# A graph-attention kernel whose edge rows come from two engines: all 31 columns of every batch fetched by GpSimd

## The chip, the cores and the metric

The kernel runs on one core of one Trainium2 chip. The metric is the device time in microseconds (us) of one execution, measured without a profiler. The profile shown here is of one further execution.

## The reference, cut to what matters

6250 nodes with 256 features and 206250 edges, sorted by destination. A layer norm, two graph-attention convolutions, a layer norm, an add, and then a mixture of 8 experts of which each node takes two.

```python
def _gat_conv(x, W, att_src, att_dst, bias, src, dst):
    xw = (x @ W).reshape(N, H, CPH)                   # N = 6250, H = 8, CPH = 16
    a_s = jnp.einsum('nhc,hc->nh', xw, att_src)
    a_d = jnp.einsum('nhc,hc->nh', xw, att_dst)
    e = jax.nn.leaky_relu(a_s[src] + a_d[dst], 0.2)
    m = jax.ops.segment_max(e, dst, num_segments=N)
    p = jnp.exp(e - m[dst])
    s = jax.ops.segment_sum(p, dst, num_segments=N)
    return jax.ops.segment_sum(xw[src] * (p / s[dst])[:, :, None], dst, num_segments=N).reshape(N, H * CPH) + bias
x = x + layernorm(concat(conv0, conv1) + layernorm(x)) * gamma + beta
x = x + top-2-of-8 experts: w * (gelu(xf @ W1[e] + b1[e]) @ W2[e] + b2[e])
```

For the change only `xw[src]` matters: for every edge, the row of its source node (128 features and 8 scores, 136 floats, 544 bytes).

## The kernel before, in words

A prologue (to some 285 us of the profile) normalises and projects all nodes, stores the rows of both convolutions in the DRAM tensor `tables`, and finds where each node's edges begin. The first 6272 edges are then done in four pieces. The other 1563 columns of 128 edges (one edge of each partition's chunk) go through 51 batches: 50 of 31 columns, the last of 13.

A batch `b` has one of three slots `G[slot(b)]` in SBUF. GpSimd (POOL) fetches its rows in `gather` (line 877), one indirect DMA of 128 rows for each column (line 882). It waits for the index list, and for the store of the batch that had the slot before, `b - 3`. VectorE (DVE) does `marks` and `scan_batch` (lines 1674 to 1713): the scores and their running maximum, the product of weights and rows (line 1701), and nine scans along the edges (1705, 1708). ScalarE (ACT) makes the exponentials (1101, 1103, 1110) and in `copy_back` (1084, 1124) turns the sums back into the slot. SyncE (SP) then issues the loads for batch `b + 3` and the store of the slot to `state` (line 661). Within an engine the order is the order of the program; between engines it is set by semaphores.

In batches 10 to 49 POOL fetches only the first 28 columns. The last three come from TensorE (PE). The table of the first convolution is loaded in SP's batch 5 (line 703) into `room`, and DVE splits it in `split_table` before batches 8 and 9 into an upper and a lower part that lie in SBUF where `X`, the node features, was. For this, SP stores `X` to DRAM (`xkept`, line 694, batches 1 to 7) and loads it again after the batches (`reload`, line 726). `code_columns` turns source nodes into codes, which SP spreads over the partitions for each batch (line 652). ACT compares them with the node numbers in `mark_stretch` (lines 1155 and 1159: 17 levels in four stretches) into one-hot matrices. PE multiplies these by the table in `columns` (line 1299): 17 levels x 3 columns x 2 parts = 102 products a batch, into three PSUM banks. DVE picks out the right third in `take_columns` (lines 1771 and 1773), nine instructions ahead of `marks`.

After the batches, POOL fetches the last state of each node (`last_states1`, `last_states2`; it waits for PE's `levels_used` before them), DVE, ACT and PE combine, normalise and route seven groups of nodes, and 105 tiles of tokens go through the experts (lines 1390 and 1396).

Of the kernel before, what the change touches and what calls it, by code (L numbers as in the profile page):

```python
# [23 lines left out]
I32 = mybir.dt.int32  # L24
ALU = mybir.AluOpType
# [50 lines left out]
FIX = 5  # L76
# [6 lines left out]
CODES_AT = 8704  # L83
# [5 lines left out]
PEC = 3  # L89
PARTS = 2  # L90
PE0, PE1 = 10, NB - 1
TABLE_AT = 5
SPLIT_AT = 8
NPC = PEC * (PE1 - PE0)
LEV = 17
TPL = 3
MIDDLE = float(LEV * P // 2)
UPPER_BITS = -(1 << 12)
SPLITS = (((0, 13), (13, 12)), ((25, 12), (37, 12)))
LEVEL_ORDER = (0, LEV - 1, *range(1, LEV - 1))  # L100
STRETCHES = ((0, 5), (5, 9), (9, 13), (13, 17))
FIX_B = 7

assert SLOTS % 2 == 1 and FIX_B + 1 < PE0 - 1
assert NBLK * BLK == E and NG * GRP == NT and (NB + NA) % NS == 1 and sum(CO) == J1 and max(CO) * 2 * ROWS <= J * ROWS
assert CL + 1 <= WA and PEC < CL and 2 * HD * WA <= HL and 2 * ROWS * WA <= ROWS * L and ZT % ZJ == 0 and ZT * P == EP
# [6 lines left out]
def build(nc, x, src, dst, W0, as0, ad0, b0, W1, as1, ad1, b1, gamma, beta, Wg, bg, eW1, eb1, eW2, eb2, out):  # L113
    ctx = ExitStack()
    with ctx:
# [20 lines left out]
        xkept = dram("xkept", [NG, P, GRP * D])  # L136
        code_type = mybir.dt.float16
        codes = dram("codes", [NPC, P], code_type)
# [7 lines left out]
        room_at = -(-(SBUF_TOP - nc.sbuf_bytes_remaining) // 32) * 32  # L146
        room = sb("room", [P, ROOM])
        arena_at = -(-(SBUF_TOP - nc.sbuf_bytes_remaining) // 32) * 32
# [13 lines left out]
        rounded = mybir.dt.float32r  # L162
        part_size = NT * ROWT
        table_parts = nc.alloc_sbuf_tensor_at("table_parts", [P, PARTS, part_size], rounded, offset=arena_at + 4 * XO, align_bytes=4)
        onehot = nc.alloc_sbuf_tensor_at("onehot", [P, LEV, PEC * P], rounded, offset=room_at, align_bytes=4)
        at = FB + PARTS * part_size - NT * D
        column_codes = [a.bitcast(code_type) for a in (AR[:, at:at + PEC * P // 2], room[:, CODES_AT:CODES_AT + PEC * P // 2])]
        assert at + PEC * P // 2 <= FB + 1152 and LEV * PEC * P <= CODES_AT and CODES_AT + PEC * P // 2 <= ROOM and LEV * TPL >= NT
# [45 lines left out]

        tile_pick = sb("tile_pick", [P, NPC, TPL])
        src_code = tile_pick.rearrange("p n q -> p (n q)")[:, 0:NPC]
        code_out = room[:, NT * ROWT:NT * ROWT + NPC // 2].bitcast(code_type)
        minus_code = sb("minus_code", [P, LEV])
# [75 lines left out]
        codes_loaded = [sem(f"codes_loaded{s}") for s in range(2)]  # L294
        levels_used = sem("levels_used")
        columns_taken = sem("columns_taken")
        parts_ready = sem("parts_ready")
        rows_copied = sem("rows_copied")
        cleared_then_node_half = sem("cleared_then_node_half")
        links_then_codes_ready = sem("links_then_codes_ready")  # L300
# [29 lines left out]
        marked_by_act = sem("marked_by_act")  # L330
# [50 lines left out]
        def by_pe(b):  # L381

            return PE0 <= b < PE1

        def pe_columns(b):

            return PEC if by_pe(b) else 0

        def fetched_columns(b):

            return cols(b) - pe_columns(b)

# [20 lines left out]
        def gather_count(b):  # L413

            return piece_count(NA - 1, slot(b)) + 16 * sum(fetched_columns(q) for q in range(b % NS, b + 1, NS))
# [50 lines left out]
        column_banks = (ps[1], ps[5], ps[6])  # L466
# [12 lines left out]

        staging = room[:, 0:part_size]  # L480
# [100 lines left out]
        def _(sp):  # L581
            with nc.allow_non_contiguous_dma(reason="small tables, once"):
# [52 lines left out]
                flat_codes = codes.rearrange("c p -> (c p)")  # L635

# [9 lines left out]
                def fetch_codes(b):  # L646
                    if b == PE0:
                        sp.wait_ge(lists_stored, 32)
                        sp.wait_ge(x_rows_stored, 16 * NG)
                        sp.wait_ge(biased_stored, 16 * NG)  # L650
                    n = PEC * (b - PE0) * P
                    sp.dma_start(column_codes[b % 2], flat_codes[n:n + PEC * P].partition_broadcast(P)).then_inc(codes_loaded[b % 2], 16)

                def fetch_and_store(b):
                    sp.wait_ge(rows_copied, NA + b + 1)
                    if by_pe(b + NS):
                        fetch_codes(b + NS)
                    if b + NS < NB:
                        fetch(b + NS)
                    s, n = slot(b), cols(b)  # L660
                    sp.dma_start(states0[:, b * J * ROWS:(b * J + n) * ROWS], G[s][:, 0:n, :].rearrange("p j r -> p (j r)")).then_inc(batch_stored[s], 16)
# [27 lines left out]
                for b in range(NB):  # L689
                    if 1 <= b < PEEL:  # L690
                        g = b - 1
                        sp.wait_ge(biased_ready, 2 * (g + 1))
                        sp.dma_start(hbd[g], norm_again.rearrange("p t d -> p (t d)")).then_inc(biased_stored, 16)
                        sp.dma_start(xkept[g], X[:, g * GRP:(g + 1) * GRP, :].rearrange("p t d -> p (t d)")).then_inc(x_rows_stored, 16)
                    if b == TABLE_AT:
                        sp.wait_ge(x_rows_stored, 16 * TABLE_AT)
                        sp.wait_ge(adstart_cleared, 16 * (ZT // ZJ))
                        sp.wait_ge(zeros_then_pads_stored, 16)
                        sp.wait_ge(adst_stored, 16)
                        for q in range(RB):  # L700
                            sp.wait_ge(row_stored[q], 16 * (-(-(NT - q) // RB)))
                        sp.wait_ge(degrees_moved_then_table_loaded, 32)
# [22 lines left out]
                def reload(g):  # L725
                    sp.dma_start(X[:, g * GRP:(g + 1) * GRP, :].rearrange("p t d -> p (t d)"), xkept[g]).then_inc(x_loaded[g], 16)

# [6 lines left out]
                for g in range(2):  # L734
                    reload(g)
# [3 lines left out]
                for g in range(NG):  # L739
# [3 lines left out]
                    if g + 2 < NG:  # L743
                        reload(g + 2)
# [6 lines left out]
                    if g >= 1:  # L751
                        sp.wait_ge(x_rows_stored, 16 * (NG + g))
# [16 lines left out]
                sp.wait_ge(x_rows_stored, 32 * NG)  # L769
# [36 lines left out]
        def _(pool):  # L806
# [15 lines left out]
            g.iota(minus_code[:, :], pattern=[[-P, LEV]], base=int(MIDDLE), channel_multiplier=-1, allow_small_or_imprecise_dtypes=True)  # L822
# [54 lines left out]
            def gather(b):  # L877
# [3 lines left out]
                for j in range(fetched_columns(b)):  # L881
# [3 lines left out]
            def gather_fix_rows(n):  # L885
                if n == 0:
                    pool.wait_ge(links_then_codes_ready, 2)
                else:
                    pool.wait_ge(fix_rows_stored, 16 * n)
# [35 lines left out]
            pool.wait_ge(levels_used, len(STRETCHES) * (PE1 - PE0))  # L925
# [49 lines left out]
        def _(act):  # L975
# [129 lines left out]
            def batch_decays(b, w=L):  # L1105
# [39 lines left out]
            def mark_stretch(b, i):  # L1145

                n, (first, end) = b - PE0, STRETCHES[i]
                if i == 0:
                    act.wait_ge(parts_ready, len(SPLITS))
                    act.wait_ge(codes_loaded[b % 2], 16 * (n // 2 + 1))  # L1150
                if n >= 1:
                    act.wait_ge(levels_used, len(STRETCHES) * (n - 1) + i + 1)
                for a in range(first, end):
                    v = LEVEL_ORDER[a]
                    last = S.activation(onehot[:, a, :], column_codes[b % 2], ACT.Abs, bias=minus_code[:, v:v + 1])  # L1155
                last.then_inc(marked_by_act, 1)
                count = 2 * (len(STRETCHES) * n + i) + 1
                act.wait_ge(marked_by_act, count)
                S.activation(onehot[:, first:end, :], onehot[:, first:end, :], ACT.Relu, bias=1.0, scale=-1.0).then_inc(marked_by_act, 1)  # L1159

            def whole_batch(b, w=L, next_w=L):
                if 1 <= b < PEEL:
                    normalise_again(b - 1)
                if b == PE0 - 1:
                    mark_stretch(b + 1, 0)
                    mark_stretch(b + 1, 1)
# [5 lines left out]
                if by_pe(b + 2) and b + 2 > PE0:  # L1172
                    mark_stretch(b + 2, 1)
# [81 lines left out]
        def _(pe):  # L1255
# [38 lines left out]
            def product(bank, mark, a, k):  # L1294

                v = LEVEL_ORDER[a]
                w = TPL * ROWT
                z = min(w, NT * ROWT - v * w)
# [962 lines left out]
```

## Time and profile before

| what | value |
|---|---|
| time, median of 3 runs | 3143.54 us (3141.79 to 3145.52) |
| span of the profiled execution | 3949.4 us |
| columns fetched by POOL in batches (line 882) | 1443 |
| columns from PE | 120 |
| busy in the span: PE, DVE, ACT, POOL | 49%, 52%, 40%, 49% |
| first gather of a batch, start of the last | 285.3 us, 2789.5 us |

The profiled execution has no other time on record than its span, which is 806 us above the median of the runs. In the rows, times are from the start of the span; "idle before" is how long the engine had been idle, and behind the arrow stands what released it. "issue" is idle time for which the profile shows no wait.

### The profile page before, as it was taken

The numbers are of one execution on the slowest core, as the hardware profiler recorded it, in microseconds if no ns is written. First come the engines' busy times: TensorE is split into PE (matmuls) and PEld (weight loads), VectorE is DVE, ScalarE is ACT, GpSimd is POOL, SyncE is SP. The second block draws the span as 40 slices with busy tenths as digits, with TensorE's granted clock in tenths as the row PEclk, the third lists the DMA queues.
The fourth block names the chain that finished last, engine by engine and source line by source line (L and its number), as shares of the span: only waits on it lengthen the run. The fifth ranks groups of instructions, "written<-read, shape, count | busy, mean of one in ns | idle before, by whom it ended". The sixth has DMA issues, their size and how long they took to land.

```text
span 3949.4 us, 38354 instructions
## 1 busy us (share of the span) xinstructions
PE 1918.5 (49%) x10116; PEld 1741.9 (44%) x10117; DVE 2043.1 (52%) x4266; ACT 1578.9 (40%) x2552; POOL 1927.4 (49%) x1920
## 2 busy tenths in 40 slices
PE   4500000134435354453544454545213489999998
PEld 2400000123425344353544453435213389999998
DVE  5465676625527355363554563545687544444443
ACT  4322223315536355453555554445323323333332
POOL 4467657645554555535555555465466612222222
PEclk8755555556767676676677776766655599999999
DMA  8244449313332333323333333233365622222222
GB/s 299 76 117 135 144 161 155 120 42 94 94 94 86 94 93 92 94 80 96 94 96 92 94 92 93 59 99 93 119 220 179 230 42 37 36 36 37 36 36 32
DMA packets 212942, 396.68 MB, mean 100 GB/s; under 512 B 76396, under 2 KB 164785, under 8 KB 206305
## 3 DMA queue, kind: packets, MB, share of 16 engines
q1 hardware_dynamic: 136049, 245.72, 18.4%
q0 software_dynamic: 75664, 149.21, 16.8%
q8 instruction: 41, 0.67, 0.1%
q10 hardware_dynamic: 1120, 0.52, 0.0%
q14 instruction: 68, 0.56, 0.0%
HBM read 203.53 MB, written 191.78 MB: 100 GB/s over the span
## 4 chain that ended last, share of the span: by engine, by line
PE 34%; issue 25%; DVE 16%; DVEq 10%; another core or an unknown queue 8%; ACT 4%; SPq 1%; POOL 1%; DMA 1%; POOLq 0%; ACTq 0%
PE ps L1299 13%; PE ps L1390 9%; PE ps L1396 9%; DVEq L1703 5%; DVE AR L1708 4%; PE ps L1270 1%; ACT onehot L1155 1%; ACT AR L1084 1%; DVEq L1709 1%; DVE AR L1773 1%; POOL AR L882 1%; DVE group_stats L1945 1%; ACT onehot L1159 1%; PE ps L1381 1%
## 5 line engine op out<-in xcount | busy, mean ns | idle before, releaser
L882 POOL DMA_INDIRECT AR<-tables,idx x1443 | 1377.0, 954 | 1095.5 <-DMA state<-AR 620.8
L1299 PE MATMUL ps<-table_parts,onehot 128*128 128x408 f32 (+1 forms) x4080 | 953.7, 388 | 1218.1 <-issue 752.5
L1299 PEld LDWEIGHTS ps<-table_parts,onehot 128*128 128x128 f32 x4080 | 861.9, 221 | 1309.9 <-issue 949.7
L1771 DVE TENSOR_SCALAR AR<-ps,tile_pick 128x136 f32<-128x136 f32 x120 | 35.4, 351 | 991.2 <-PE ps L1299 555.4
L1084 ACT COPY AR<-AR 128x1984 f32<-128x1984 f32 (+3 forms) x110 | 392.0, 3564 | 355.1 <-DVE AR L1708 195.6
L956 POOL DMA_INDIRECT out<-AR,idb x105 | 183.5, 1748 | 597.6 <-issue 560.1
L1708 DVE TENSOR_TENSOR_SCAN AR<-ps,AR 128x512 f32<-128x512 f32 x404 | 454.2, 1197 | 0.0
L1390 PEld LDWEIGHTS ps<-AR 128*128 128x128 f32 x3360 | 393.9, 193 | 6.6 <-DVE AR L2164 1.3
L1390 PE MATMUL ps<-AR 128*128 128x128 f32 x3360 | 394.5, 276 | 0.9 <-DVE AR L2164 0.9
L1701 DVE TENSOR_TENSOR AR<-AR,ps 128x3968 f32<-128x3968 f32 (+1 forms) x51 | 356.7, 6994 | 20.7 <-ACT AR L1103 13.4
L1101 ACT ACTIVATE ps<-AR 128x248 f32<-128x248 f32 (+1 forms) x51 | 19.2, 376 | 702.4 <-DVE AR L1688 411.4
L1155 ACT ACTIVATE onehot<-AR,minus_code 128x384 fp32r<-128x384 f16 x340 | 180.2, 603 | 265.6 <-remote 253.7
L2164 DVE COPY AR<-AR 128x1024 f32 x210 | 151.4, 721 | 208.7 <-PE ps L1390 207.2
L1159 ACT ACTIVATE onehot<-onehot 128x1536 fp32r<-128x1536 f32 (+1 forms) x160 | 250.6, 1566 | 5.1
L1243 ACT ACTIVATE AR<-ps,bcur 128x128 f32<-128x128 f32 x424 | 121.2, 369 | 258.6 <-PE ps L1390 258.5
L1243 ACT ACTIVATE room<-ps,bcur 128x128 f32<-128x128 f32 x416 | 119.0, 368 | 254.1 <-PE ps L1390 254.1
L1155 ACT ACTIVATE onehot<-room,minus_code 128x384 fp32r<-128x384 f16 x340 | 180.1, 604 | 67.1 <-remote 59.0
L1396 PE MATMUL ps<-AR 128*128 x848 | 191.9, 379 | 1.3 <-DVE AR L2207 1.3
L1396 PE MATMUL ps<-AR,room 128*128 x832 | 188.2, 379 | 0.0
L1396 PEld LDWEIGHTS ps<-AR 128*128 128x128 f32 x848 | 157.0, 190 | 20.8 <-issue 1.7
L1396 PEld LDWEIGHTS ps<-AR,room 128*128 128x128 f32 x832 | 154.0, 190 | 18.8
L1326 PE MATMUL ps<-ident,sml 128*128 128x128 f32 x6 | 2.4, 501 | 319.7 <-DVE sml L1845 319.7
(345 smaller groups left out, 2352.4 us busy)
## 6 DMA issues: line engine op xcount, KB each, us to landing
state<-AR SPq DMA_DIRECT2D x50, 2232.0 KB
AR<-tables,idx POOLq DMA_INDIRECT x1492
AR<-in_L_ffn_W SPq DMA_DIRECT2D x16, 1024.0 KB
AR<-placed SPq DMA_DIRECT2D x105, 130.0 KB, 2.0
adstart<-room SPq DMA_DIRECT2D x26, 496.0 KB
AR<-adstart SPq DMA_DIRECT2D x50, 248.0 KB
tables<-AR SPq DMA_DIRECT2D x49, 136.0 KB
room<-tables SPq DMA_DIRECT2D x14, 476.0 KB
```

Source lines behind the costliest of these rows:

```text
L882: pool.indirect_dma_start(out=G[s][:, j, 0:ROWT], out_offset=None, in_=table_rows, in_offset=bass.IndirectOffsetOnAxis(ap=idx[:, s, j:j + ...
L956: pool.indirect_dma_start(out=out, out_offset=bass.IndirectOffsetOnAxis(ap=idb[:, s, :], axis=0), in_=ys[:, s, :], in_offset=None, bounds_ ...
L1084: return S.copy(to.rearrange("p j (h c) -> p j h c", h=HD)[:, :, :, a:z], of[:, :, 1:n + 1].rearrange("p (c h) j -> p j h c", h=HD)[:, :, ...
L1155: last = S.activation(onehot[:, a, :], column_codes[b % 2], ACT.Abs, bias=minus_code[:, v:v + 1])
L1159: S.activation(onehot[:, first:end, :], onehot[:, first:end, :], ACT.Relu, bias=1.0, scale=-1.0).then_inc(marked_by_act, 1)
L1243: last = S.activation(hsT[s][:, m, :], ps[2 * s + h][:, (m % 4) * P:(m % 4 + 1) * P], ACT.Gelu, bias=bcur[:, s, m:m + 1])
L1299: return T.matmul(bank[:, 0:z], mark, table_parts[:, k, v * w:v * w + z], start=(a == 0 and k == 0), stop=(a == LEV - 1 and k == PARTS - 1))
L1390: mm = T.matmul(ps[2 * s + h][:, m * P:(m + 1) * P], w1_cur[:, k, (h * 4 + m) * P:(h * 4 + m + 1) * P], xsT[:, s, k, :], start=(k == 0), s ...
L1396: mm = T.matmul(ps[5][:, 0:D], hsT[s][:, m, :], AR[:, bass.ds(e * (MH * D) + (NEX * KD * HID + m * D), D)], start=(m == 0), stop=(m == MH ...
L1701: V.tensor_tensor(TS[:, 0:F, js].rearrange("p (c h) j -> p c h j", h=HD), rows_in[:, :, 0:F].rearrange("p j (h c) -> p c h j", h=HD), bc(W ...
L1703: dd()
L1708: V.tensor_tensor_scan(T2[:, i * step:(i + 1) * step], decays(w), T2[:, i * step:(i + 1) * step], 0.0, ALU.mult, ALU.add).then_inc(entry_u ...
```

## The change

`by_pe`, `pe_columns` and `fetched_columns` go, and `gather` issues `cols(b)` indirect DMAs in every batch. `mark_stretch`, `product`, `columns`, `code_columns`, `take_columns`, `split_table` and every call and semaphore of theirs go. `X` stays in its place in SBUF: its store to `xkept` and its reload go, and the loads of the table and of the codes. The order of all that remains is as before.

```diff
-                for j in range(fetched_columns(b)):
+                for j in range(cols(b)):
                     pool.indirect_dma_start(out=G[s][:, j, 0:ROWT], out_offset=None, in_=table_rows,
...
-            return piece_count(NA - 1, slot(b)) + 16 * sum(fetched_columns(q) for q in range(b % NS, b + 1, NS))
+            return piece_count(NA - 1, slot(b)) + 16 * sum(cols(q) for q in range(b % NS, b + 1, NS))
...
                     sp.wait_ge(rows_copied, NA + b + 1)
-                    if by_pe(b + NS):
-                        fetch_codes(b + NS)
                     if b + NS < NB:
...
                         sp.dma_start(hbd[g], norm_again.rearrange("p t d -> p (t d)")).then_inc(biased_stored, 16)
-                        sp.dma_start(xkept[g], X[:, g * GRP:(g + 1) * GRP, :].rearrange("p t d -> p (t d)")).then_inc(x_rows_stored, 16)
-                    if b == TABLE_AT:
...
-                        sp.dma_start(staging.rearrange("p (t r) -> p t r", r=ROWT), tab[0].rearrange("(t p) r -> p t r", p=P)).then_inc(degrees_moved_then_table_loaded, 16)
-                    if b == FIX + 1:
-                        sp.wait_ge(links_then_codes_ready, 3)
-                        sp.dma_start(codes.rearrange("c p -> p c"), code_out).then_inc(lists_stored, 16)
                     if b == NB - 1:
-                        sp.wait_ge(levels_used, len(STRETCHES) * (PE1 - PE0))
...
-            pool.wait_ge(levels_used, len(STRETCHES) * (PE1 - PE0))
             for n in range(4):
                 last_states2(n)
...
-                if by_pe(b + 1):
-                    mark_stretch(b + 1, 2)
-                    mark_stretch(b + 1, 3)
...
-                    if half == 0 and by_pe(b + 2) and b + 2 > PE0:
-                        mark_stretch(b + 2, 0)
...
-                if by_pe(b + 2) and b + 2 > PE0:
-                    mark_stretch(b + 2, 1)
...
-            pe.wait_ge(parts_ready, len(SPLITS))
-            for b in range(PE0, PE1):
-                for i in range(len(STRETCHES)):
-                    columns(b, i)
             chain(2)
...
             def whole_batch(b, w=L, next_w=L):
-                if SPLIT_AT <= b < SPLIT_AT + len(SPLITS):
-                    split_table(b - SPLIT_AT)
-                if by_pe(b):
-                    take_columns(b)
...
-                    if g + 2 < NG:
-                        reload(g + 2)
...
-                dve.wait_ge(x_loaded[g], 48 if g == NG - 1 else 32)
+                dve.wait_ge(x_loaded[g], 32 if g == NG - 1 else 16)
```

## Rows read from the trace of the kernel before

**Rows 1.** The page: busy time of each engine, share of the span, instructions.
```profile
PE 1918.5 (49%) x10116; PEld 1741.9 (44%) x10117; DVE 2043.1 (52%) x4266; ACT 1578.9 (40%) x2552; POOL 1927.4 (49%) x1920
```

**Rows 2.** Who waited for whom, whole span: us in total, times, longest.
```profile
PE ps L1299 <- issue: 752.5, 322, 54.2
...
POOL AR L882 <- DMA state<-AR: 620.8, 24, 58.1
...
DVE AR L1771 <- PE ps L1299: 555.4, 18, 89.4
```

**Rows 3.** Line 882: ns min/median/max; idle before it; who waited for it.
```profile
L882 POOL DMA_INDIRECT AR<-tables,idx x1443: 942/947/2572, 285.3 to 2789.5; - x181
...
  issue: 474.6, 1419
...
  DVE AR L1680: 4.5, 1
```

**Rows 4.** POOL in order of time: start, us, instruction, idle before.
```profile
743.26 2.55 POOL L882 DMA_INDIRECT AR<-tables,idx  x1 [0.30 <-issue]
...
848.44 0.95 POOL L882 DMA_INDIRECT AR<-tables,idx  x1 [0.30 <-issue]
849.69 0.94 POOL L882 DMA_INDIRECT AR<-tables,idx  x1 [0.30 <-issue]
908.72 0.94 POOL L882 DMA_INDIRECT AR<-tables,idx  x1 [58.08 <-DMA state<-AR]
...
1003.35 0.95 POOL L882 DMA_INDIRECT AR<-tables,idx  x1 [24.89 <-DMA state<-AR]
```

**Rows 5.** PE in order of time: products that come singly, and in a run.
```profile
814.82 0.50 PE L1299 MATMUL ps<-table_parts,onehot 128*128 128x408 f32 x1 [2.30 <-issue]
817.62 0.50 PE L1299 MATMUL ps<-table_parts,onehot 128*128 128x408 f32 x1 [2.30 <-issue]
...
866.84 21.05 PE L1299 MATMUL ps<-table_parts,onehot 128*128 128x408 f32 x102 [3.01 <-DVE AR L1773]
```

**Rows 6.** DVE in order of time: batches 10 and 12.
```profile
871.28 0.41 DVE L1692 COPY AR<-ps 128x248 f32<-128x248 f32 x1
...
872.67 7.25 DVE L1701 TENSOR_TENSOR AR<-AR,ps 128x3968 f32<-128x3968 f32 x1
...
931.64 6.98 DVE L1701 TENSOR_TENSOR AR<-AR,ps 128x3968 f32<-128x3968 f32 x1 [0.63 <-issue]
```

**Rows 7.** All engines in order of time: batches 3, 4 and 5, with 31 fetched columns.
```profile
505.18 6.80 DVE L1701 TENSOR_TENSOR AR<-AR,ps 128x3968 f32<-128x3968 f32 x1
...
525.19 1.03 ACT L1124 COPY AR<-AR 128x496 f32<-128x496 f32 x1
...
545.78 6.80 DVE L1701 TENSOR_TENSOR AR<-AR,ps 128x3968 f32<-128x3968 f32 x1
...
580.03 6.79 DVE L1701 TENSOR_TENSOR AR<-AR,ps 128x3968 f32<-128x3968 f32 x1
```

**Rows 8.** DVE in order of time, behind batch 0.
```profile
379.55 0.28 DVE L1830 TENSOR_SCALAR fix_at<-fix_at 128x1 f32<-128x1 f32 x3 [5.87 <-issue]
```

**Rows 9.** POOL and DVE in order of time, around the end of the batches.
```profile
2820.30 0.95 POOL L919 DMA_INDIRECT room<-state,node_index  x1 [29.90 <-PE ps L1299]
...
2860.31 0.17 DVE L1672 COPY carry<-AR 128x16 f32<-128x16 f32 x1
```

**Rows 10.** SyncE in order of time: the store of batch 12's slot.
```profile
994.24 0.43 SPq L661 DMA_DIRECT2D state<-AR  x1
```

**Rows 11.** The chain that ended last, a piece of the combining stage.
```profile
3117.10 13.12 another core or an unknown queue
```

**Rows 12.** Groups of instructions: busy us, mean ns, idle before.
```profile
L1159 ACT ACTIVATE onehot<-onehot 128x1536 fp32r<-128x1536 f32 (+1 forms) x160 | 250.6, 1566 | 5.1
...
L1790 DVE TENSOR_TENSOR table_parts<-room 128x1632 fp32r<-128x1632 f32 (+1 forms) x4 | 7.5, 1884 | 0.0
...
L2069 DVE TENSOR_TENSOR AR<-AR 128x1792 f32<-128x1792 f32 x7 | 14.2, 2026 | 0.5
```

More of the change, by code:

```diff
@@ L75 @@
 AW = 38048
-FIX = 5
 BIASED_IN = ((0, 2), (0, 2), (1, 2), (1, 2), (2, 1), (3, 2), (3, 2))
@@ L82 @@
 ROOM = 9088
-CODES_AT = 8704
 AHEAD = 2 * GRP
@@ L88 @@
 ZFIRST = 14
[L89 to L101, printed above, removed]
 FIX_B = 7
-assert SLOTS % 2 == 1 and FIX_B + 1 < PE0 - 1
+assert SLOTS % 2 == 1 and FIX_B + 2 < NB - 2
 assert NBLK * BLK == E and NG * GRP == NT and (NB + NA) % NS == 1 and sum(CO) == J1 and max(CO) * 2 * ROWS <= J * ROWS
-assert CL + 1 <= WA and PEC < CL and 2 * HD * WA <= HL and 2 * ROWS * WA <= ROWS * L and ZT % ZJ == 0 and ZT * P == EP
+assert CL + 1 <= WA and 2 * HD * WA <= HL and 2 * ROWS * WA <= ROWS * L and ZT % ZJ == 0 and ZT * P == EP
 def bc(ap, shape):
@@ L135, in build @@
         placed = dram("placed", [NEX * REG + P + 2 * P, ROWP])
-        xkept = dram("xkept", [NG, P, GRP * D])
-        code_type = mybir.dt.float16
-        codes = dram("codes", [NPC, P], code_type)
         states0 = state[0][NP:EP, :].rearrange("(p j) r -> p (j r)", p=P)
@@ L143, in build @@
         adstart_c = adstart[NP:EP, :].rearrange("(p j) r -> p (j r)", p=P)
-        room_at = -(-(SBUF_TOP - nc.sbuf_bytes_remaining) // 32) * 32
         room = sb("room", [P, ROOM])
-        arena_at = -(-(SBUF_TOP - nc.sbuf_bytes_remaining) // 32) * 32
         AR = sb("AR", [P, AW])
@@ L160, in build @@
         FB = XO + NT * D
[L162 to L168, printed above, removed]
         zero = room[:, 0:1024]
@@ L213, in build @@
         bcur = sb("bcur", [P, 2, MH])
[L215 to L218, printed above, removed]
         hrow = room[:, 5520:6032].rearrange("p (s d) -> p s d", s=2)
@@ L293, in build @@
         searched_by_act = sem("searched_by_act")
[L294 to L297, printed above, removed]
         rows_copied = sem("rows_copied")
         cleared_then_node_half = sem("cleared_then_node_half")
-        links_then_codes_ready = sem("links_then_codes_ready")
+        links_ready = sem("links_ready")
         last_states_spread = sem("last_states_spread")
@@ L329, in build @@
         places_ready = sem("places_ready")
-        marked_by_act = sem("marked_by_act")
         pads_then_tiles_ready = sem("pads_then_tiles_ready")
@@ L379, in build @@
             assert any(GRP * (g + 1) - 1 in counted_at(t) for t in range(count_step(g))) or g == 0
[L381 to L391, printed above, removed]
         def slot(b):
@@ L465, in build @@
         same = cut(5820, C)
-        column_banks = (ps[1], ps[5], ps[6])
         VIEW = {}
@@ L478, in build @@
         degree_rows = share_of.rearrange("p a b c t h -> p (a b c t h)")[0:NT, 0:P]
-        staging = room[:, 0:part_size]
         def repeats(w):
@@ L633, in _ @@
                     load_piece_adst(q)
-                flat_codes = codes.rearrange("c p -> (c p)")
                 def fetch_adst(b):
@@ L644, in fetch @@
                     fetch_adst(b)
[L646 to L652, printed above, removed]
                 def fetch_and_store(b):
                     sp.wait_ge(rows_copied, NA + b + 1)
-                    if by_pe(b + NS):
-                        fetch_codes(b + NS)
                     if b + NS < NB:
@@ L693, in _ @@
                         sp.dma_start(hbd[g], norm_again.rearrange("p t d -> p (t d)")).then_inc(biased_stored, 16)
-                        sp.dma_start(xkept[g], X[:, g * GRP:(g + 1) * GRP, :].rearrange("p t d -> p (t d)")).then_inc(x_rows_stored, 16)
-                    if b == TABLE_AT:
[L696 to L702, printed above, removed]
-                        sp.dma_start(staging.rearrange("p (t r) -> p t r", r=ROWT), tab[0].rearrange("(t p) r -> p t r", p=P)).then_inc(degrees_moved_then_table_loaded, 16)
-                    if b == FIX + 1:
-                        sp.wait_ge(links_then_codes_ready, 3)
-                        sp.dma_start(codes.rearrange("c p -> p c"), code_out).then_inc(lists_stored, 16)
                     if b == NB - 1:
-                        sp.wait_ge(levels_used, len(STRETCHES) * (PE1 - PE0))
                         for i in range(NOWN):
@@ L723, in down_in @@
                     sp.dma_start(w2s[:, e, :, :], eW2[e].rearrange("(m p) d -> p m d", p=P)).then_inc(expert_weights_loaded, 16)
-                def reload(g):
-                    sp.dma_start(X[:, g * GRP:(g + 1) * GRP, :].rearrange("p t d -> p (t d)"), xkept[g]).then_inc(x_loaded[g], 16)
                 own(3)
@@ L733, in _ @@
                 own(5)
-                for g in range(2):
-                    reload(g)
                 for g in (5, 6):
@@ L751, in _ @@
                     if g >= 1:
-                        sp.wait_ge(x_rows_stored, 16 * (NG + g))
+                        sp.wait_ge(x_rows_stored, 16 * g)
                     sp.dma_start(out[g * GRP * P:(g + 1) * GRP * P, :].rearrange("(t p) d -> p t d", p=P), X[:, g * GRP:(g + 1) * GRP, :]).then_inc(x_rows_stored, 16)
@@ L767, in _ @@
                 sp.dma_start(placed[NEX * REG:NEX * REG + P, :], padrow[:, :]).then_inc(zeros_then_pads_stored, 16)
-                sp.wait_ge(x_rows_stored, 32 * NG)
+                sp.wait_ge(x_rows_stored, 16 * NG)
                 for i in range(3):
@@ L821, in _ @@
             g.iota(e8[:, :], pattern=[[1, HD]], base=0, channel_multiplier=0, allow_small_or_imprecise_dtypes=True)
-            g.iota(minus_code[:, :], pattern=[[-P, LEV]], base=int(MIDDLE), channel_multiplier=-1, allow_small_or_imprecise_dtypes=True)
             g.memset(padrow[:, :], 0.0)
@@ L886, in gather_fix_rows @@
                 if n == 0:
-                    pool.wait_ge(links_then_codes_ready, 2)
+                    pool.wait_ge(links_ready, 2)
                 else:
@@ L1143, in _ @@
                 copy_piece_back(q)
[L1145 to L1159, printed above, removed]
             def whole_batch(b, w=L, next_w=L):
@@ L1163, in whole_batch @@
                     normalise_again(b - 1)
-                if b == PE0 - 1:
-                    mark_stretch(b + 1, 0)
-                    mark_stretch(b + 1, 1)
                 batch_weights(b, w)
@@ L1292, in _ @@
             project(NT - 1)
[L1294 to L1298, printed above, removed]
-                return T.matmul(bank[:, 0:z], mark, table_parts[:, k, v * w:v * w + z], start=(a == 0 and k == 0), stop=(a == LEV - 1 and k == PARTS - 1))
-            def columns(b, i):
-                n, (first, end) = b - PE0, STRETCHES[i]
-                if i == 0 and n >= 1:
-                    pe.wait_ge(columns_taken, n)
-                pe.wait_ge(marked_by_act, 2 * (len(STRETCHES) * n + i + 1))
-                for a in range(first, end):
-                    for c in range(PEC):
-                        for k in range(PARTS):
-                            mm = product(column_banks[c], onehot[:, a, c * P:(c + 1) * P], a, k)
-                mm.then_inc(levels_used, 1)
             pe.wait_ge(edge_lists_used, 1)
@@ L1321, in chain @@
                 pe.wait_ge(last_states_spread, n + 1)
-                pe.wait_ge(links_then_codes_ready, 1)
+                pe.wait_ge(links_ready, 1)
                 if n >= 1:
@@ L1518, in edge_marks @@
                 V.tensor_copy(dstF, dstI)
-                V.tensor_copy(src_code[:, :].rearrange("p (b c) -> p b c", c=PEC),
-                              srcI[:, PE0 * J:PE1 * J].rearrange("p (b j) -> p b j", j=J)[:, :, J - PEC:J])
                 V.tensor_copy(dst1[:, :], idx1[:, 1, :])
@@ L1733, in _ @@
             edge_columns(VIEW[L, HD])
-            def code_columns():
-                tile, of_level, at_ = cut(0, NPC), cut(NPC, NPC), cut(2 * NPC, NPC)
-                dd()
-                V.tensor_scalar(tile, src_code[:, :], 1.0 / P, 0.5 / P - 0.5, ALU.mult, ALU.add)
-                dd()
-                V.tensor_scalar(tile, tile, MAGIC, None, ALU.add)
-                dd()
-                V.tensor_scalar(tile, tile, MAGIC, None, ALU.subtract)
-                dd()
-                V.tensor_scalar(of_level, tile, 1.0 / TPL, -1.0 / TPL, ALU.mult, ALU.add)
-                V.scalar_tensor_tensor(at_, tile, -float(P), src_code[:, :], ALU.mult, ALU.add)
-                dd()
-                V.tensor_scalar(of_level, of_level, MAGIC, None, ALU.add)
-                dd()
-                V.tensor_scalar(of_level, of_level, MAGIC, None, ALU.subtract)
-                dd()
-                V.tensor_scalar(at_, at_, MIDDLE, None, ALU.subtract)
-                dd()
-                V.scalar_tensor_tensor(code_out, of_level, float(P), at_, ALU.mult, ALU.add).then_inc(links_then_codes_ready, 1)
-                V.scalar_tensor_tensor(tile, of_level, -float(TPL), tile, ALU.mult, ALU.add)
-                dd()
-                for q in range(TPL):
-                    V.tensor_scalar(tile_pick[:, :, q], tile, float(q), None, ALU.is_equal)
-                dd()
@@ L1761, in take_columns @@
-            def take_columns(b):
-                dve.wait_ge(batch_stored[slot(b)], free_count(b))
-                dve.wait_ge(levels_used, len(STRETCHES) * (b - PE0 + 1))
-                for q in range(TPL):
-                    for c in range(PEC):
-                        to = G[slot(b)][:, cols(b) - PEC + c, 0:ROWT]
-                        n = PEC * (b - PE0) + c
-                        pick, of = tile_pick[:, n, q:q + 1], column_banks[c][:, q * ROWT:(q + 1) * ROWT]
-                        if q == 0:
-                            last = V.tensor_scalar(to, of, pick, None, ALU.mult)
-                        else:
-                            last = V.scalar_tensor_tensor(to, of, pick, to, ALU.mult, ALU.add)
-                    if q == TPL - 1:
-                        last.then_inc(columns_taken, 1)
-                    dd()
@@ L1778, in split_table @@
-            def split_table(k):
-                if k == 0:
-                    dve.wait_ge(degrees_moved_then_table_loaded, 48)
-                    dve.wait_ge(x_rows_stored, 16 * NG)
-                    dve.wait_ge(biased_stored, 16 * NG)
-                for first, n in SPLITS[k]:
-                    a, z = first * ROWT, (first + n) * ROWT
-                    upper = room[:, part_size:part_size + n * ROWT]
-                    V.tensor_scalar(upper.bitcast(I32), staging[:, a:z].bitcast(I32), UPPER_BITS, None, ALU.bitwise_and)
-                    dd()
-                    V.tensor_copy(table_parts[:, 0, a:z], upper)
-                    last = V.tensor_tensor(table_parts[:, 1, a:z], staging[:, a:z], upper, ALU.subtract)
-                    dd()
-                last.then_inc(parts_ready, 1)
@@ L1823, in _ @@
             dd()
-            V.tensor_tensor(sml[:, 8:10], sml[:, 2:4], sml[:, 4:6], ALU.mult).then_inc(links_then_codes_ready, 1)
+            V.tensor_tensor(sml[:, 8:10], sml[:, 2:4], sml[:, 4:6], ALU.mult).then_inc(links_ready, 1)
             V.tensor_scalar(fix_skip[:, :], sml[:, 2:4], -1.0, -float(SKIP), ALU.add, ALU.mult)
@@ L1833, in _ @@
             V.tensor_tensor(fix_index[:, 1, 0:2], fix_at[:, 0:2], fix_skip[:, :], ALU.add)
-            V.tensor_tensor(fix_index[:, 1, 2:3], fix_at[:, 2:3], fix_skip[:, 1:2], ALU.add).then_inc(links_then_codes_ready, 1)
+            V.tensor_tensor(fix_index[:, 1, 2:3], fix_at[:, 2:3], fix_skip[:, 1:2], ALU.add).then_inc(links_ready, 1)
             V.scalar_tensor_tensor(own_score[:, :, :], scores[:, :, 2 * HD:], 0.2, scores[:, :, 2 * HD:], ALU.mult, ALU.max)
@@ L1926, in _ @@
                     spread_lasts(1)
-                if b == FIX:
-                    code_columns()
                 if b == FIX_B - 2:
```

## The prediction

> **What bounds the kernel now.** I read the page first. No engine is busy for more than 52% of the span, and POOL, PE and DVE are all about half busy [rows 1], so shares of busy time decide nothing. The table of waits comes next. Its largest entries are PE waiting 752.5 us for "issue" and, behind it, POOL waiting 620.8 us for a slot's store and DVE waiting 555.4 us for PE's columns [rows 2]. Nobody waits for a fetched row except once, for 4.5 us [rows 3]. Taken as it stands, the profile says that TensorE's columns bound the batches and that fetching is free. The change would then be a large gain.
>
> But the span is 3949.4 us and the runs take 3143.54. Something in the profiled execution costs 806 us that the runs don't have, so I looked for it in order of time. Around 815 us the products of line 1299 come singly, 2.8 us apart, with no semaphore in between; from 866.84 on, 102 of them come in one run of 21.05 us [rows 5]. Waits of the same kind stand on DVE where PE does nothing: three 128x1 instructions come 5.87 us late [rows 8]. I take these waits for the recording of the execution. They are in the span and, by the 806 us, mostly not in the runs. So the question is what bounds a batch when PE isn't held up.
>
> That can be seen where batches follow undisturbed. Batches 10 and 12, whose rows were all fetched beforehand, start their product (line 1701) at 872.67 and 931.64: 59.0 us for two, 29.5 us a batch for PE, ACT and DVE together, `take_columns` included [rows 6]. POOL's gathers start 1.25 us apart, 0.947 busy and a pause of 0.30 [rows 4]; the pause is there 1419 times, 474.6 us in all [rows 3]. 28 of them take 35.0 us. That is above 29.5, so in the runs POOL should bound the batches, and nothing else.
>
> **Does that add up to the runs?** From the first gather's start (285.3) to the end of the last (2789.5 + 0.9) the profile has 2505 us [rows 3]. 1443 gathers without a break take 1443 x 1.25 = 1804. That takes 701 us off the span: 3248. The last batch's last sum (2860.31) stands 70 us behind the last gather, because batch 49 waited for a PE that was held up; POOL itself lost 29.90 us to it [rows 9]. In step it would be about 25 us: batch 49's gathers end 16 us (13 gathers) before, 6 us of short instructions and 17 of product and scans follow, and batch 50 is a short one of some 14. That is 45 less: 3203. The missing 60 us would be waits of the recording in the prologue and the combining stage, where the chain alone holds a piece of 13.12 us that no wait explains [rows 11]. So 1.25 us a gather fits. Were none of these 105 us artefacts, the gathers would have to be faster: (1804 - 105) / 1443 = 1.18 us. I keep 1.18 and 1.25 as the bounds of a gather's price in the runs and take 1.25, which the rows show.
>
> **The change part by part.**
> - Added: 3 gathers in each of 40 batches, 120 on the engine that bounds: 120 x 1.25 = +150 us (120 x 1.18 = +142 at the lower bound). A batch goes from 35.0 to 38.75 us.
> - What must keep up with that: without columns, a batch takes 21.0 us on DVE and ACT from the start of line 1701 (505.18) to the end of the copies (526.2) [rows 7], and the short instructions from line 1692 to the next product take 1.4 (871.28 to 872.67) [rows 6]: 22.4 us a batch against 38.75. A slot is free again some 6 + 21 + 1 us after its last row, and the store behind that: batch 12's was issued at 994.24 [rows 10] and POOL went on at 1003.35 [rows 4], 9.1 us. That makes 37 us, where two batches of gathers (77.5 us) lie in between. Nothing else becomes late; POOL runs without a break.
> - Removed from PE: 102 products a batch, 21 us [rows 5]. They lay beside POOL's 35 us: 0.
> - Removed from ACT: 17 comparisons and 4 ramps a batch; the ramps alone are 6.3 us (4 x 1.566) [rows 12]. Removed from DVE: nine short instructions. Both are covered by POOL's time: 0. If that cover were gone they would be worth at most 29.5 - 22.4 = 7 us a batch.
> - `split_table`: 7.5 us in its slowest line [rows 12], its other two lines about as much again, spread over batches 8 and 9; `code_columns` less than 5 us in batch 5. A batch with the bias work took 34.3 us undisturbed (545.78 to 580.03) [rows 7], and batch 8 has none of it, so 22.4 + 8 stays below 38.75: 0.
> - `xkept`, its reload, the loads of table and codes: 7 x 2 x 896 KB and 3.3 MB less to move. The reader of the reloaded rows, line 2069, is idle before it for 0.5 us in seven instructions [rows 12], so no reload was late: 0, and up to 5 us of a gain from freer queues.
> - POOL's wait for `levels_used` goes. Its 29.90 us in the profile [rows 9] come from the held-up PE. In step, PE is done with batch 49 before POOL is: 0.
>
> **The port that POOL shares.** The gather at 743.26 took 2.55 us instead of 0.947 [rows 4], at the time of `split_table`. Over all 1443 gathers the mean is 954 ns and the median 947 [rows 3], so all such delays together are 10 us. I take 7 of them as due to the table and off POOL's path with it: -7 us (bounds 0 and -10). The Trainium skill, "SBUF — State Buffer", in its part on the "DVE blocks DMA" trap, says that a DMA issued by GpSimd is starved of descriptors while VectorE holds the shared port pair with a copy in a two-port mode. By that rule the slow gathers are VectorE's doing and the change frees POOL wherever such copies go; the trace agrees in kind, but leaves it only the 10 us.
>
> **Sum.** 3143.5 + 150 - 7 = 3287 us, +4.6%. Against the profiled execution's own span the same steps come out the other way: PE's 8160 instructions leave the record, and most of the waits named above with them. I expect a span of about 3450 us, 500 shorter than before, while the runs get 143 us longer.
>
> **Rivals.**
> - *The column loop, not POOL, sets the pace of the runs.* For it: the table of waits [rows 2]. If all 806 us came out of the gathers from 743.3 to 2789.5 (2046 us, 1133 gathers), they would stand 1.09 us apart and a batch would take 30.6 us, near the 29.5 seen. The 0.30 us pause would be recording as well, and the gathers might be faster still. With 1.00 to 1.09 us the changed batches take 31.0 to 33.8 us: +16 to +128, in the middle 3215. Against it: the pause is the same in quiet stretches and in loaded ones, and other stretches have waits of the same kind [rows 8, 11], so not all 806 us lie here.
> - *The same loop with gathers fast enough: faster than before.* If the pause vanished and a gather took its busy time alone, 0.947, a changed batch would take 31 x 0.947 = 29.4 us where the column loop had 30.6: 40 x -1.2 = -48, about 3095 us. It decides from a gather below 30.6 / 31 = 0.99 us. Against it: at that price the rest of the span could hold no artefact at all.
> - *The early batches show what 31 columns cost.* Batch 3 to 4 took 40.6 us [rows 7], others up to 45, not 38.75. If transfers slowed that stretch, 40 batches at 43 instead of 35 us are +320: 3460 us. Against it: the delay is on DVE and of the kind of [rows 8], and the next batch took 34.3 [rows 7].
>
> **How the numbers follow.** Forecast 0.82, column loop 0.08, column loop with fast gathers 0.05, early batches 0.05. About 0.2% (6 us) is what a measurement of this kernel can tell from no change. Faster by more than that: the second rival, 0.05. Within: a strip of the first, 0.02. Slower: 0.93. The forecast's own range is 3270 to 3300: from 142 - 10 with 5 more gained, to 150 with nothing gained and some us of other effects. I widen it downwards, toward the first rival: 3240 to 3308.
>
> **What would show it.** In the new trace: 1563 gathers, still 1.25 us apart; 38.7 us between the first gathers of neighbouring batches, with no wait for a store after the first ten; DVE waiting for rows (line 1680) some 10 us a batch, where before it waited for PE; a shorter span and a longer time. The prediction is wrong if POOL still waits for stores in the middle of the batches, or if gathers stand at another distance.

## The result, and the profile after

| | before | after |
|---|---|---|
| time, median | 3144.25 us (3141.79 to 3145.52) | 3286.65 us (3284.73 to 3289.11) |
| span of the profiled execution | 3949.4 us | 3283.0 us |
| first gather to the end of the last | 2505.1 us, 1443 gathers | 1968.1 us, 1563 gathers |
| before the first, behind the last | 285, 1159 us | 236, 1079 us |

The median before is now of four runs. The changed kernel takes 1.0457 times as long, 95% interval [1.0442, 1.0472]: 142.4 us more. The forecast was 3287. The span went the other way, by 666 us.

The page of the kernel after. The busy shares answer to [rows 1], and the last two lines are the chain of work that ended last, by engine and by line:

```profile
PE 953.1 (29%) x6036; PEld 872.1 (27%) x6037; DVE 1908.2 (58%) x3880; ACT 977.7 (30%) x1712; POOL 2046.2 (62%) x2039
...
POOL 4777777777777777777777777777773222222222
...
POOL 48%; PE 24%; issue 16%; DVE 6%; DMA 2%; DVEq 1%; ACT 1%; SPq 0%; POOLq 0%; ACTq 0%
POOL AR L797 45%; PE ps L1255 11%; PE ps L1261 11%; DMA tables<-AR 1%; POOL room L834 1%; PE ps L1246 1%; DVE group_stats L1743 1%; POOL adstart L757 1%; ACT AR L1091 1%; DVE AR L1524 1%; POOL placed L861 1%; DMA AR<-in_dst,node_index 0%; DVE AR L1867 0%; DVE AR L1864 0%; DVE AR L1803 0%
```

POOL is busy 7 tenths in every slice of the batches, without a dip, and the gathers (line 882 before, 797 now) are 45% of the chain. That a bound engine shows 7 and not 9 is the pause of 0.30 us between two gathers: 0.95 in 1.25.

The gathers themselves, answering to [rows 3]: ns min/median/max, idle before, who waited.

```profile
L797 POOL DMA_INDIRECT AR<-tables,idx x1563: 943/947/2482, 236.1 to 2203.2; - x196
...
  issue: 476.0, 1561
  DMA state<-AR: 2.1, 1
...
  DVE AR L1543: 721.2, 50
```

The only waits but the pause are one of 2.1 us for a store and one of 0.3. DVE now waits for rows 50 times, 14.4 us each, where it had waited once. One batch on all engines, in order of time, shows it:

```profile
1202.55 0.98 POOL L797 DMA_INDIRECT AR<-tables,idx  x1 [0.31 <-issue]
1203.84 0.95 POOL L797 DMA_INDIRECT AR<-tables,idx  x1 [0.30 <-issue]
...
1205.85 1.04 ACT L1033 COPY AR<-AR 128x496 f32<-128x496 f32 x1
...
1220.13 0.57 DVE L1543 TENSOR_TENSOR AR<-AR,ps 128x248 f32<-128x248 f32 x1 [15.71 <-DMA AR<-tables,idx]
...
1224.24 6.80 DVE L1564 TENSOR_TENSOR AR<-AR,ps 128x3968 f32<-128x3968 f32 x1
...
1244.26 1.02 ACT L1033 COPY AR<-AR 128x496 f32<-128x496 f32 x1
...
1258.94 0.57 DVE L1543 TENSOR_TENSOR AR<-AR,ps 128x248 f32<-128x248 f32 x1 [16.07 <-DMA AR<-tables,idx]
```

DVE starts on one batch's rows at 1220.13 and on the next one's at 1258.94, 38.8 us apart, which is 31 gathers at 1.25. From the product (1224.24) to the last copy's end (1245.28) are 21.0 us, as in [rows 7]; most of the rest is waiting for rows.

### The profile page after: what moved, and what is told of

Its sections match the earlier page's. It is cut to its first block, busy times and chain, and to the rows that moved or that the text cites. A ratio compares the mean times of both kernels' runs of the same rounds, so it can differ in the third digit from the quotient of the medians.

```text
span 3283.0 us, 28765 instructions
## 1 busy us (share of the span) xinstructions
PE 953.1 (29%) x6036; PEld 872.1 (27%) x6037; DVE 1908.2 (58%) x3880; ACT 977.7 (30%) x1712; POOL 2046.2 (62%) x2039
## 4 chain that ended last, share of the span: by engine, by line
POOL 48%; PE 24%; issue 16%; DVE 6%; DMA 2%; DVEq 1%; ACT 1%; SPq 0%; POOLq 0%; ACTq 0%
POOL AR L797 45%; PE ps L1255 11%; PE ps L1261 11%; DMA tables<-AR 1%; POOL room L834 1%; PE ps L1246 1%; DVE group_stats L1743 1%; POOL adstart L757 1%; ACT AR L1091 1%; DVE AR L1524 1%; POOL placed L861 1%; DMA AR<-in_dst,node_index 0%; DVE AR L1867 0%; DVE AR L1864 0%; DVE AR L1803 0%
## 5 line engine op out<-in xcount | busy, mean ns | idle before, releaser
L797 POOL DMA_INDIRECT AR<-tables,idx x1563 | 1486.7, 951 | 478.3 <-issue 476.0
L1543 DVE TENSOR_TENSOR AR<-AR,ps 128x248 f32<-128x248 f32 (+1 forms) x51 | 28.8, 564 | 721.3 <-DMA AR<-tables,idx 721.2
L1564 DVE TENSOR_TENSOR AR<-AR,ps 128x3968 f32<-128x3968 f32 (+1 forms) x51 | 343.0, 6726 | 0.0
L2003 DVE TENSOR_TENSOR AR<-ps,room 128x256 f32<-128x256 f32 x105 | 44.6, 425 | 152.3 <-PE ps L1261 152.3
L861 POOL DMA_INDIRECT placed<-AR,ipos x98 | 104.8, 1069 | 41.4 <-issue 28.4
L750 POOL DMA_INDIRECT AR<-in_dst,node_index x49 | 47.0, 958 | 50.7 <-DVE node_index L1357 37.3
L1158 PE MATMUL ps<-AR,room 128*128 128x304 f32 x196 | 69.8, 484 | 12.5 <-ACT room L906 12.3
```

The source lines that it names most:

```text
L750: pool.indirect_dma_start(out=blkrow[t % AHEAD].bitcast(I32), out_offset=None, in_=dblk, in_offset=bass.IndirectOffsetOnAxis(ap=node_index ...
L797: pool.indirect_dma_start(out=G[s][:, j, 0:ROWT], out_offset=None, in_=table_rows, in_offset=bass.IndirectOffsetOnAxis(ap=idx[:, s, j:j + ...
L861: pool.indirect_dma_start(out=placed, out_offset=bass.IndirectOffsetOnAxis(ap=ipos[:, n % 2, k, t:t + 1], axis=0), in_=pr[n % 4][:, t, :], ...
L1158: mm = T.matmul(ps[2 + t % 2][:, 0:WR], hT[:, t % 2, k * P:(k + 1) * P], Wc[:, k, :], start=(k == 0), stop=(k == KD - 1))
L1564: V.tensor_tensor(TS[:, 0:F, js].rearrange("p (c h) j -> p c h j", h=HD), rows_in[:, :, 0:F].rearrange("p j (h c) -> p c h j", h=HD), bc(W ...
```

## The experiments

"Over before" is the difference from the kernel before in the same job, whose median was 3141.26 in e1 to e4, 3139.5 in e5 to e8 and 3142.38 in e9 to e11.

**e1: all column work kept, but in vain.** It starts from the kernel before.

```diff
-            return cols(b) - pe_columns(b)
+            return cols(b)
...
+                if b == PE0:
+                    dve.wait_ge(fix_rows_stored, 32)
...
-                        to = G[slot(b)][:, cols(b) - PEC + c, 0:ROWT]
+                        to = (carry, padrow, fix_row)[c][:, 0:ROWT]
```

> The kernel before, with all column work of TensorE, ScalarE and VectorE left in, but GpSimd fetches all 31 columns of every batch and VectorE puts the three computed columns into spare tiles instead of the slot. Theory (POOL alone bounds the batches, the column work lies beside it): a batch takes 31 x 1.25 = 38.75 us whatever the others do, so the time is that of the kernel after, 3287 us, plus 0 to 10 for the table's traffic and split: 3287 to 3297. Rival (the column loop costs the runs time of its own, as the waits on PE in the old profile say): then removing it gained something in the kernel after, and this one is clearly slower than that: above 3310. Rival (faster gathers under a column loop of 30.6 us): this one would be at or below 3215.

Measured: 3288.57 us (3287.49 to 3290.45), 147.3 over before. With 120 more gathers and everything else in place the kernel before becomes as slow as the kernel after (142.4 and 143.0 over before), and 4 to 5 us slower still, for which see e7. Line 1299 and its companions cost the runs next to nothing: e3 below, of the same job, has none of them and is 0.7 us from this.

**e2: the three columns not fetched at all.** It starts from the kernel after.

```diff
+            return 28 if 10 <= b < NB - 1 else cols(b)
...
-                for j in range(cols(b)):
+                for j in range(fetched(b)):
```

> The kernel after, with only the first 28 columns of batches 10 to 49 fetched; the last three hold what the slot held before, so this leaves 120 fetches out. No column work at all. Theory: 120 x 1.25 = 150 us less than the kernel after, 3137 us, which is the kernel before (3144) less the few us of its table and split: the column work of the kernel before costs nothing. Rival (column loop sets the pace before): this one, free of the loop, is faster than the kernel before by more than 20 us. Rival (gathers at 1.18 us or less): 3145 or above.

Measured: 3133.4 us (3131.45 to 3134.66), 7.9 below before, ratio 0.9977 [0.9967, 0.9986]. Against the kernel after (143.0 over before in e6) 120 gathers are worth 150.9 us: 1.257 each. The two differences are from two jobs; what such differences vary by is seen in the kernel after (142.4 and 143.0) and in e3 and e7 (146.7 and 148.2). So all of TensorE's column path together, with its table, cost the kernel before 8 us.

**e3 and e7: x and the table moved and split, but no columns.** The codes are made and stored here, but not loaded for each batch (line 652). From the kernel before:

```diff
-            return PE0 <= b < PE1
+            return False
...
-            for b in range(PE0, PE1):
-                for i in range(len(STRETCHES)):
-                    columns(b, i)
...
-                if b == PE0 - 1:
-                    mark_stretch(b + 1, 0)
-                    mark_stretch(b + 1, 1)
```

> The kernel after, with x stored and loaded again, the table loaded and split, and the codes made, stored, but no one-hots, no products and no columns taken. Theory, by the step of the prediction that put -7 us on the split's hold on GpSimd: 7 us above the kernel after, 3294; bounds 0 and +10 (and up to 5 more from the traffic). Rival: nothing at all, within 2 us of the kernel after, if the slow gathers of the old trace were recording too.

> The kernel of e3 again, beside the kernel after: stores and reloads of x, table load, split and codes, without columns. The prediction's step says +7 us (0 to 10) over the kernel after; the first run of it, against another chip's kernel after, said about +1 to +4. I expect +3, inside the noise or just out of it. By the mean of a gather in its trace (953 against 951 ns, 1563 gathers) it would be +3.

Measured: 3287.92 (3286.99 to 3289.35), 146.7 over before, in e3; 3287.7 (3286.68 to 3291.21) in e7, beside the kernel after, **e6**, at 3282.53 (3281.47 to 3283.93). The ranges of e6 and e7 don't meet: +5.2 us.

> The kernel after, unchanged, on the same chip as the next run, to compare with it: 3284 to 3287 us.

e6 is 143.0 over before, ratio 1.0457 [1.0443, 1.0471].

e7's trace shows slow gathers where `split_table` runs, ten of them with 5.8 us above the ordinary 0.945. POOL and DVE in order of time (the split's lines are 1778, 1780 and 1781 there, 881 is the gather):

```profile
586.03 1.08 DVE L1780 CAST table_parts<-room 128x1768 fp32r<-128x1768 f32 x1
586.38 1.55 POOL L881 DMA_INDIRECT AR<-tables,idx  x1 [0.30 <-issue]
587.03 1.99 DVE L1781 TENSOR_TENSOR table_parts<-room 128x1768 fp32r<-128x1768 f32 x1
588.24 1.99 POOL L881 DMA_INDIRECT AR<-tables,idx  x1 [0.30 <-issue]
```

**e9: the same without split_table.**

```diff
-                if SPLIT_AT <= b < SPLIT_AT + len(SPLITS):
-                    split_table(b - SPLIT_AT)
```

> The kernel of e3 and e7 (x stored and loaded again, table and codes loaded) without split_table. The kernel after is 143.0 us above the kernel before of its job, that of e7 148.2. Theory (the 5 us are ten gathers held up by the split's VectorE instructions, 5 to 6 us of excess in the trace at 585 to 632 us): this one is 143 above, within 2. Rival (the 5 us are the traffic of x and of the table): 148.

Measured: 3285.83 us (3283.53 to 3286.71), 143.4 over before, ratio 1.0457 [1.0443, 1.0471]. In its trace the ten slow gathers are gone, and only those beside the additions of beta (see e10) are left. So the 5 us are the split; e7 and e9 are from two jobs, their medians only 1.9 us apart, and it is the difference to the kernel before and the gathers in the traces that say so. The traffic of x and of the table costs nothing that can be seen. The loads of the codes, which the expectation counts in, are in none of e3, e7 and e9, but in e1, where they cost nothing either.

**e10: beta in PSUM.** From the kernel after:

```diff
-        beta_spread = bet[:, :]
+        beta_spread = ps[6][:, 0:D]
...
             V.tensor_copy(bias_spread, b01[:, :])
+            V.tensor_copy(beta_spread, bet[:, :])
```

> The kernel after with beta spread in PSUM instead of SBUF, so that the addition of beta to x in batches 1 to 7 reads one operand from PSUM. In the traces each of the seven such additions has a gather beside it of 1.6 to 2.7 us, 8 to 9 us of excess in all, while the addition of the biases just ahead of it, with one operand in PSUM, has none. Theory (two operands in SBUF hold GpSimd's descriptors up): 8 to 9 us less than the kernel after, so about 134.5 above the kernel before. Rival (any long VectorE instruction that writes SBUF does it): no change, 143.

Measured: 3276.24 us (3274.64 to 3278.96), 133.9 over before: 9.2 less than the kernel after in e6, another job. The traces agree: from the first gather's start to the last one's are 1964.8 us in e6 and 1955.5 in e10, and seven gathers with 9.4 us above the ordinary in all are gone. First the kernel after, then e10, in order of time, at the addition of beta (line 1707; the gather is 797):

```profile
311.13 2.06 DVE L1707 TENSOR_TENSOR AR<-AR,bet 128x1792 f32<-128x1792 f32 x1
311.13 0.95 POOL L797 DMA_INDIRECT AR<-tables,idx  x1 [0.30 <-issue]
312.38 1.62 POOL L797 DMA_INDIRECT AR<-tables,idx  x1 [0.30 <-issue]
```

```profile
312.38 2.01 DVE L1707 TENSOR_TENSOR AR<-AR,ps 128x1792 f32<-128x1792 f32 x1
313.09 0.94 POOL L797 DMA_INDIRECT AR<-tables,idx  x1 [0.30 <-issue]
314.34 0.94 POOL L797 DMA_INDIRECT AR<-tables,idx  x1 [0.30 <-issue]
```

The same addition, equally long, holds a gather up with both operands in SBUF, and doesn't with one in PSUM. The rival, that any long VectorE instruction that writes SBUF does it, is out: this one still writes SBUF.

**e8: only 16 columns fetched.** As e2, with 16 for 28.

> The kernel after with only 16 columns of batches 10 to 49 fetched; the other 15 hold what the slot held, so this leaves 600 fetches out. GpSimd would need 20.0 us a batch. Theory: here the loop of VectorE and ScalarE takes over, 22.4 us a batch (21.0 from product to the end of the copies and 1.4), so 40 x (38.75 - 22.4) = 654 us less: 2633 us. If GpSimd still bounded: 750 less, 2537. If the loop were the 29.5 us that the column work had: 2917.

Measured: 2632.94 us (2632.6 to 2633.69), 649.6 less than e6 of the same job. The loop of DVE and ACT is the next bound. In the trace DVE doesn't wait for rows in these batches, and POOL waits for the store of a slot once a batch, 39 times in a row. Two such waits:

```profile
1215.81 0.94 POOL L801 DMA_INDIRECT AR<-tables,idx  x1 [1.09 <-DMA state<-AR]
...
1239.08 0.94 POOL L801 DMA_INDIRECT AR<-tables,idx  x1 [3.61 <-DMA state<-AR]
```

These two are 23.3 us apart; over all 39 (671.95 to 1531.89) the mean is 22.6. That is the loop's price, 0.2 above the expected 22.4.

**e5: the kernel before, recorded once more.**

> The kernel before, unchanged, for a second profile of it. Theory (the 806 us in the first profile are the recording's, which waits to be written out when the record is dense): with 38354 instructions recorded again, the span is again far above the runs, near 3950. Rival (that one recorded execution was disturbed, and the four-column kernel with its 41154 instructions and a span of 3086.5 us against 3088.8 shows that the density isn't the cause): span 3140, gathers 1.25 us apart without a break, VectorE waiting for rows (line 1680) about 6 us a batch, and hardly for TensorE. Now I hold the rival likelier, 0.75.

Measured: 3140.19 us, one run, span 3138.4. Its largest waits of PE and DVE in the batches, and then its gathers:

```profile
PE ps L1299 <- ACT onehot L1159: 580.6, 105, 86.1
...
DVE AR L1680 <- DMA AR<-tables,idx: 434.8, 50, 15.2
```

```profile
L882 POOL DMA_INDIRECT AR<-tables,idx x1443: 938/944/2640, 236.1 to 2057.9; - x181
...
  issue: 439.2, 1441
  DMA state<-AR: 2.8, 1
```

The wait of PE for "issue", the largest of [rows 2], is gone. So are POOL's waits for stores, but for one of 2.8 us, and DVE's for PE's columns. Gathers run without a break, and DVE waits for rows 8.7 us a batch. This is the profile from which the result could have been read at once.

**e4: four columns from TensorE.** From the kernel before:

```diff
-PEC = 3
+PEC = 4
...
-        column_banks = (ps[1], ps[5], ps[6])
+        column_banks = (ps[1], ps[5], ps[6], ps[0])
```

> The kernel before with four columns a batch from TensorE instead of three (a fourth PSUM bank), so GpSimd fetches 27: 33.75 us a batch. Theory: POOL bounds until the column loop is longer. PE 136 x 0.206 = 28 us, ScalarE 10.3 + about 20 = 31 us, VectorE 26; the loop of 29.5 us seen with three columns grows by some 4 on ScalarE and 1 on VectorE, to 33 or 35. If it stays below 33.75: 3144 - 50 = 3094. If it is 35: 3144. So 3094 to 3144, best guess 3105. Rival (the column loop already bounds with three): slower than before, by 40 x 4 = 160: 3300.

Measured: 3088.78 us (3088.23 to 3091.17), 52.5 below before, ratio 0.9837 [0.9822, 0.9852]. That is better than the expected 3094 to 3144 (best guess 3105): the column loop didn't grow to 33 or 35 us. PE in order of time, from one batch to the next, and DVE's waits for rows:

```profile
1215.12 26.57 PE L1299 MATMUL ps<-table_parts,onehot 128*128 128x408 f32 x136 [3.79 <-DVE AR L1773]
1245.49 14.67 PE L1299 MATMUL ps<-table_parts,onehot 128*128 128x408 f32 x72 [3.79 <-DVE AR L1773]
...
DVE AR L1680 <- DMA AR<-tables,idx: 283.9, 49, 10.5
```

30.4 us for the column loop where nothing holds it, 33.75 for POOL: POOL still bounds, by 3.4 us. A fifth column would add some 6.6 us to PE by estimate (34 products of 0.195), and the loop would pass POOL's 32.5. It wasn't tried; the one-hots would be 17 x 5 x 128 = 10880 values, where the kernel has room for 8704.

**e11: both, four columns and beta in PSUM**, which is the best version.

> The kernel of e4 (four columns from TensorE) with beta in PSUM as in e10: e4 was 52.5 us below the kernel before; with 8 to 9 us less, 61 below, ratio 0.9807. If the early batches have slack, 52.5 still.

Measured: 3084.58 us (3082.8 to 3085.28), 57.8 below before, ratio 0.9814 [0.9801, 0.9828]: 5.3 us of the hoped 8 to 9. In its trace the gathers beside the beta additions are all ordinary. Those beside the split are as slow as before (6.8 us above ordinary in all). Its gathers take 5.8 us less from the first start to the last than in e4 (1765.4 against 1771.2). Why the rest of the 8 to 9 us isn't there stays open.

## Why the prediction was right

- **POOL at 28 x 1.25 = 35.0 us bounds the batches of the runs.** Right. Shown by e1 (PE's work in vain costs nothing beyond the split, more gathers cost everything), e2 (PE's work removed gains 8 us) and e5.
- **+150 for 120 gathers.** Measured 150.9 (e2 against e6). The choice of 1.25 over 1.18 was right: the pause of 0.30 is the same in every trace and isn't recording.
- **-7 for the split.** Measured 5.2 (e7 against e6, and e9 takes them away). The traces have 5.8 us of excess in the gathers around it (e7). The size came out near by some luck: I had all delays of gathers at 10 us and gave the table 7 of them, while e5's trace has some 15, about 9 of them beside the additions of beta, which the change leaves. Of the 8 us that e2 finds, some 3 remain for all the rest of the column work. 150.9 - 7.9 = 143.0 is e6.
- **0 for PE, ACT, `take_columns` and traffic.** Right (e1, e9). The figure of 22.4 us for the loop without columns was near: 22.6 in e8's trace. That e8 took 2632.94 where 2633 was expected is luck in part: 654 us were to be saved, and against e6 of its own job it saves 649.6.
- **The 806 us.** That they weren't in the runs was right, and the sum leaned on nothing else. The cause that I gave was wrong. I took them for waits that recording itself brings, and expected the changed kernel's span near 3450, because PE's 8160 instructions leave it; it was 3283.0. e5 records the same 38354 instructions in 3138.4 us, and e4 41154 in 3086.5. That one recorded execution was disturbed, and no number of instructions explains it. What disturbed it stays open.
- **The bookkeeping of the artefacts.** I put 105 us outside the gathers (45 behind the last, 60 elsewhere). From e5: the part before the first gather lost 49 (285.3 to 236.1) and the part behind the last 79 (1159 to 1080), 128 in all. The gathers, which I had at 1804, take 1823, as some are slow. The two misses cancel.
- **DVE waits some 10 us a batch for rows.** It is 14.4. The 10 didn't follow from my own terms: 38.75 - 22.4 is 16.

No rival survives. The column loop would have put e1 above 3310, or e2 more than 20 us below before; fast gathers would have put e1 at 3215; and for the early batches, whose first gathers are 38.8 to 41.4 us apart in the kernel after, the 43 us of that rival don't come: from batch 10 on it is 38.8 throughout.

The port's rule was right in kind, and e10 says more than I had made of it. About 2.02 us of an addition with both inputs in SBUF delay a gather by 0.7 to 1.8 us (1.62 us in the trace of the kernel after, up to 2.75 in e6, for 0.945), and with one input in PSUM by nothing. The Trainium skill, "SBUF — State Buffer", under "Who interferes with whom", names a second case beside the fast copies: a VectorE instruction with two SBUF inputs contends with a GpSimd instruction that reads SBUF. The delays here agree with that. The same section says that a `tensor_tensor` wasn't seen to stall a DMA, and infers that making descriptors doesn't need the port it takes; here a `tensor_tensor` does hold up POOL's indirect DMA, and the measurement decides.

## What to carry to other kernels

Compare the span with the runs before reading a single wait. If they differ, look for a stretch where nothing is held up and read the period of each loop there; the loop with the longest undisturbed period is the bound. Then price a change by that loop alone (here 1.25 us for each gather issued). Work moved off that engine is nearly free as long as its own loop stays shorter, and the gap between the two (here 35.0 against 29.5) says that more can be moved: one more column gave 52 us.

## What the runs showed of the hardware that I had not expected

- An execution may be recorded with a span 26% above its runs, with single products 2.8 us apart on PE and pauses on other engines, and the same program again at its true length (3949.4 and 3138.4 us).
- An indirect gather of 128 rows costs POOL 0.944 to 0.947 us (the medians) and 0.30 of pause in all traces, with PE busy for 82% of the batches (e4) or idle (after). In e5, e6, e7 and e10 every gather above 1.05 us lies beside a DVE instruction with all inputs in SBUF; not every such instruction lengthens one. Removing seven such delays gave 9.2 us.
- TensorE's granted clock from 700 to 2000 us was 0.50, the lower of its two levels (1.2 and 2.4 GHz), with no column (PE idle), 0.81 with three (e5, PE busy 64%) and 0.90 with four (e4, 82%), so at the higher level for most of the time. With four, 136 products took 26.57 us, 0.195 each.
